# Scaling the softmax numerators of a two-layer transformer kernel on ScalarE in place of VectorE

## The reference

```python
# layer 0 attention: one head of width 1024, scores kept on and above the diagonal
q, k, v = split(x @ W)
s = triu(q @ k.T / sqrt(1024));  s = where(s == 0, -9e15, s)      # zeros are masked too
y = softmax(s) @ v
# layer 0 feed-forward: activations to 8 bits, weights ternary, GELU between
# layer 1 attention: 8 query heads of 128, 2 key/value heads, keys and values
#   through a latent of 32, causal (on and below the diagonal), output matrix wo
# layer 1 feed-forward: as in layer 0, without bias
out = x + LN(ffn1(LN(x)))
```

## Time and profile before

| | us |
|---|---|
| median of 3 runs (lowest, highest) | 11456.64 (11453.26, 11465.77) |
| profiled execution: its own time | 11503.57 |
| profiled execution: span of the slowest core, from which all rows are | 11501.7 |
| spans of the eight cores | 11419.8 to 11501.7 |
| mean granted PE clock of that core, share of 2.4 GHz | 0.691 |

### The profile page before, as it was taken

One profiled execution on the slowest core, in us unless ns is written; L12 is line 12 of the kernel. 1 busy time (PEld: TensorE's weight loads), 2 busy tenths in 40 slices (PEclk: granted clock), 3 DMA queues, 4 the chain that ended last, 5 costly groups with the idle time before them and its releaser, 6 DMA issues.

```text
span 11501.7 us, 87492 instructions; the slowest of 8 cores (11419.8 to 11501.7 us)
## 1 busy us (share of the span) xinstructions
PE 5184.4 (45%) x24204; PEld 2362.5 (21%) x24204; DVE 4585.1 (40%) x10726; ACT 3401.8 (30%) x5060; POOL 1.0 (0%) x7
## 2 busy tenths in 40 slices
PE   3444555413333325663333444455555244443666
PEld 1111222101111113331111122222222111111333
DVE  2222232234444443222234556666666422234222
ACT  1111112233444432111223333333433344443111
POOL 0000000000000000000000000000000000000000
PEclk8777766655666667886666666666666577775888
DMA  2111001141000022222000000000000311113222
GB/s 70 37 37 53 23 23 32 37 129 37 33 33 33 33 102 93 76 73 70 29 20 22 15 15 12 12 12 8 8 8 8 128 42 39 39 39 143 73 73 73
DMA packets 159419, 530.52 MB, mean 46 GB/s; under 512 B 49316, under 2 KB 65764, under 8 KB 137447
## 3 DMA queue, kind: packets, MB, share of 16 engines
q1 hardware_dynamic: 158952, 524.93, 13.4%
HBM read 373.88 MB, written 150.99 MB: 46 GB/s over the span
## 4 chain that ended last, share of the span: by engine, by line
PE 38%; DVE 24%; ACT 16%; issue 9%; DMA 6%; DVEq 3%; ACTq 3%; SPq 0%; POOL 0%; PEldq 0%; POOLq 0%
PE psO L1501 9%; PE psS L1315 8%; PE psT L165 5%; PE psS L402 4%; DVE pp L519 3%; PE psO L749 3%; DVE negmh L434 3%; PE psO L1024 3%; ACTq L1251 3%; PE psS L585 2%; DVE fam L1340 2%; ACT pp L462 2%; ACT hbuf L1375 2%; DMA wtmp<-w 2%; DVE ppT L1042 2%
## 5 line engine op out<-in xcount | busy, mean ns | idle before, releaser
L337 ACT ACT_TABLE_LOAD x128 | 164.2, 1283 | 3003.8 <-DVE st L320 3003.8
L1315 PE MATMUL psS<-wq1T,xqT 128*128 128x512 bf16 x4096 | 1031.9, 418 | 41.2 <-ACT hbuf L1369 26.5
L1501 PE MATMUL psO<-wq2T,hqT 128*128 128x512 bf16 x4096 | 1007.8, 412 | 67.3 <-DVE hqT L1486 67.3
L165 PE MATMUL psT<-identb,pp 128*128 128x128 bf16 x4752 | 538.6, 250 | 957.1 <-DVE pp L519 957.1
L165 PE MATMUL psT<-identb,xq 128*128 128x128 bf16 x512 | 64.8, 307 | 1688.8 <-DVE xq L1237 1688.8
L434 DVE TENSOR_REDUCE negmh<-psS 128x1 f32<-128x512 f32 (+3 forms) x900 | 571.7, 647 | 320.7 <-PE psS L402 303.4
L462 ACT ACTIVATE pp<-psS,negmh 128x512 bf16<-128x512 f32 (+3 forms) x900 | 580.6, 648 | 225.2 <-DVE negmh L434 215.0
L165 PEld LDWEIGHTS psT<-identb,pp 128*128 128x128 bf16 x4752 | 414.9, 112 | 1112.3 <-issue 1059.9
L402 PE MATMUL psS<-kl,qTb 128*128 128x512 bf16 (+3 forms) x792 | 393.9, 511 | 551.5 <-ACT pp L462 526.3
L1042 DVE COPY ppT<-psT 128x512 bf16<-128x512 bf16 x1056 | 448.1, 425 | 370.5 <-PE psT L165 345.8
L1315 PEld LDWEIGHTS psS<-wq1T,xqT 128*128 128x128 bf16 x4096 | 433.2, 107 | 615.7 <-issue 229.8
(11 more groups left out here) (162 smaller groups left out, 8284.8 us busy)
## 6 DMA issues: line engine op xcount, KB each, us to landing
wtmp<-w SPq DMA_DIRECT2D x128, 512.0 KB, 4.3
h_q<-hq SPq DMA_DIRECT2D x64, 1024.0 KB, 4.7
wtmp<-w SPq DMA_DIRECT2D x32, 2048.0 KB, 8.1
hqs<-h_q SPq DMA_DIRECT2D x64, 1024.0 KB, 5.8
xres<-xst SPq DMA_DIRECT2D x96, 512.0 KB, 2.9
xa<-xres SPq DMA_DIRECT2D x96, 512.0 KB, 5.5
xst<-xres SPq DMA_DIRECT2D x96, 512.0 KB, 3.8
xa<-x SPq DMA_DIRECT2D x32, 512.0 KB, 3.3
```

Source lines behind the costliest of these rows:

```text
L165: return te.matmul(out_ap, in_ap, self.identb[:], is_transpose=True, start=start, stop=stop, skip_group_check=True)
L1315: last = t.matmul(me.psS[:, hf * 512:hf * 512 + 512], B["xqTp"][:, dc * 128:dc * 128 + 128], wq1T[:, dc * HID + k * 512:dc * HID + k * 512 ...
L1501: last = t.matmul(me.psO[:, e * 512:e * 512 + 512], hqT[:, p * 4096 + hc * 128:p * 4096 + hc * 128 + 128], wq2T[:, hc * 1024 + e * 512:hc ...
```

## The change

The multiplication of `fac` by `rden` and the scaling of `pp` move from DVE to ACT, as `activation` with the function Identity, an immediate bias of 0 and a per-partition scale read from SBUF. The reciprocal now raises `v`, ACT waits for that count, and ACT's last scaling raises `s`. `flash_rows` hands back which semaphore and which count say that `pp` is ready, and the transposes wait for these. The number of instructions, their shapes, and the tiles that they read and write stay the same; so does everything outside this part of `flash_rows` and that wait.

```diff
+        rdone = me.cnt["v"] + 1
+
         @blk.scalar
         def _(s):
             me.w(s, "v", vdone)
             me.mark(s.activation(out=me.fac[:, 0:N], in_=me.fac[:, 0:N],
                                  func=AF.Exp, bias=0.0, scale=-1.0), "s")
-        sdone = me.cnt["s"]
+            s.wait_ge(me.semh["v"], rdone)
+            s.drain()
+            for r in range(R):
+                s.activation(out=me.fac[:, r * nb:r * nb + nb],
+                             in_=me.fac[:, r * nb:r * nb + nb],
+                             func=AF.Identity, bias=0.0,
+                             scale=me.rden[:, r:r + 1])
+            s.drain()
+            iv = None
+            for r in range(R):
+                pp_row = rows[r][1]
+                for c in range(nb):
+                    wdt = min(512, klen - 512 * c)
+                    iv = s.activation(out=pp_row[:, 512 * c:512 * c + wdt],
+                                      in_=pp_row[:, 512 * c:512 * c + wdt],
+                                      func=AF.Identity, bias=0.0,
+                                      scale=me.fac[:, r * nb + c:r * nb + c + 1])
+            me.mark(iv, "s")
+        sdone = me.cnt["s"] - 1
+        ppmark = me.cnt["s"]
...
-            v.reciprocal(out=me.rden[:, 0:R], in_=me.rden[:, 0:R])
-            v.drain()
-            for r in range(R):
-                v.tensor_scalar(out=me.fac[:, r * nb:r * nb + nb],
-                                in0=me.fac[:, r * nb:r * nb + nb],
-                                scalar1=me.rden[:, r:r + 1], scalar2=None,
-                                op0=ALU.mult)
-            v.drain()
-            iv = None
-            for r in range(R):
-                pp_row = rows[r][1]
-                for c in range(nb):
-                    wdt = min(512, klen - 512 * c)
-                    iv = v.tensor_scalar(out=pp_row[:, 512 * c:512 * c + wdt],
-                                         in0=pp_row[:, 512 * c:512 * c + wdt],
-                                         scalar1=me.fac[:, r * nb + c:r * nb + c + 1],
-                                         scalar2=None, op0=ALU.mult)
-            me.mark(iv, "v")
+            iv = v.reciprocal(out=me.rden[:, 0:R], in_=me.rden[:, 0:R])
+            assert me.mark(iv, "v") == rdone
+        return ("s", ppmark)
...
-                    self.flash_rows(
+                    ppsem, ppready = self.flash_rows(
...
-                    ppready = me.cnt["v"]
...
-                                    me.w(t, "v", ppready)
+                                    me.w(t, ppsem, ppready)
```

## The result

The change makes the kernel slower: 11902.74 us, the median of 8 runs (11887.18 to 11930.87), against 11455.94 us, the median of 8 runs of the kernel before on the same chip (11433.76 to 11484.11). The ratio is 1.0394, 95% interval 1.038 to 1.0408. The medians differ by 447 us where 460 were forecast; the time was forecast at 11,917 with a range of 11,850 to 12,040. The profiled execution has a span of 11898.9 us on its slowest core; it is only 397 us above the span of before, 11501.7 us, because the profiled execution of before lay 48 us over its median.

A forecast was written before the change was run, and what follows sets the result against it. No engine was taken as the bound, but a chain of handoffs with the scaling bare on it. Scaling 432, rescaling 20 and handoff 7 made 460 us more (rounded), on 11456.6: 11,917 us, range 11,850 to 12,040.

The forecast's parts named there:

- The scaling stands alone: Scaling of pp before the transposes: bare path, PE and ACT idle meanwhile; DVE's 334.6 us all lie on the path.
- The price of a step: Scaling of pp on ACT: 0.62 us from start to start, 767 us in all, 432 us more than on DVE.
- The Trainium skill's price: Scaling of pp on ACT, priced by the skill's page: 613 ns a block, an end at about 11,907 us.
- The small terms: Rescaling of fac on ACT, 20 us more, and the handoff from DVE's reciprocal to ACT, 7 us more.
- No table load: Identity on ACT needs no table load; the rival load would add 123 us, 12,040 us, chance 0.04.
- no clock: Transposes after the longer pause: no clock cost; the rival of PE staying at 1.2 GHz gave 12,147 us, chance 0.02.
- One sign: Transposes of the last call: PE would show 1.2 GHz (0.50) for 5 to 6 us, then 2.4 GHz (1.00).
- The overlap: Successive scalings on ACT overlap; the rival without overlap had a step of 0.722 us and 12,039 us, chance 0.06.
- The other side: Rival at the transposes: PE released while ACT still scales, about 11,150 us if fully hidden, chance 0.01.
- the turning point: In the early-release rival: it decides once 460 of ACT's 767 us are hidden, 60%.

The follow-up runs named there:

- e3_no_scaling: The changed kernel with the scaling of pp and the drain before it left out (computes something else): 11137.09 us, 0.9728 of the kernel before.
- e2_no_pointer: The changed kernel with an immediate scale of 1.0 instead of the pointer into fac (computes something else): 11771.86 us, 1.0287 of the kernel before.
- e1_fac_dve: The changed kernel with the small rescaling of fac back on DVE, the scaling of pp still on ACT: 11869.30 us, 1.0369 of the kernel before.
- e5_early_dve: The kernel before, scaling on DVE by column block ahead of its copies, each transpose group waiting for its own block: 11413.92 us, ratio 0.9973.

## Why the prediction was right

**The scaling stands alone.** It said that every microsecond of the step is bare path because nobody has anything else to do. The wait grew by 447.5 us and the medians by 447, and e3_no_scaling gave the other proof: 766.0 us of wait gone, and 758 to 766 us of time with it.

**The price of a step.** The prediction took 0.62 us from rows of other functions with other sources; it is 0.613. The term is 759.4 us for 767, and 425 us more than on DVE for 432. Two small errors stand behind the step, and partly cancel: one scaling lasts 709 ns for 722, because the GELU row gave 629 ns without a pointer where Identity on bf16 takes 615, and neighbours overlap by 709 - 613 = 96 ns where the sum had 722 - 620 = 102. The pointer's 93 ns were right, for one scaling (709 - 615 = 94) and in the chain (613 - 520 = 93 in e2_no_pointer). The Trainium skill's price, from its page ScalarE: Activation LUTs, section What ACT_TABLE_LOAD costs, was 613 ns a step, and the estimate by it an end at about 11,907 us. The trace agrees with the step to the nanosecond, and the estimate is 4 us off.

**The small terms.** Rescaling and handoff were put at 27 us. The wait's 447.5 less the 425 of the scaling leaves 22 to 23: the rescaling took 65.3 us on ACT for 46.9 on DVE, 18 us more where 20 were forecast, and some 4 are left for the handoff, where 7 were. e1_fac_dve returned 20.0 us of wait for both. The terms were slightly too high, by 7 us for the scaling and by 4 to 5 for the small ones; with the rounding that is the 13 us by which the sum is above the measured difference.

**No table load, no clock.** 96 loads at each of the two lines, as before. One sign was not met as written: the stretch at 1.2 GHz in the last call is 3.5 us after a pause of 27.1 us, where 5 to 6 were named from the 6.0 after 15.5. The prediction had read two calls, and single calls vary from about 3 to above 6 us in both kernels. What it rested on holds: over all phases of layer 1 the time at 1.2 GHz went from 292 to 301 us, and the phases have the same length within 3 us, all by the medians of the cores. Both rivals were dropped by the trace alone, the clock's by e3_no_scaling too.

**The overlap.** With no overlap the step would have been 0.709; the same tile read and written in place did not stop it.

**The other side.** The rival that PE might be let go early did not occur, for the reason given. Built on purpose it showed its worth: at 0.9907 with ACT's scaling the rival's mechanism is real. 580 of the 766 us were hidden there, 76% where 60% was named as the turning point. Its price of 11,150 us was too low, because it let nothing of the first block show; with the first block on DVE 11,230 was reached.

## What to carry to other kernels

Ask of a step not which engine has room for it but what runs beside it: on a chain of handoffs with nothing beside it, an engine that is 10 points less busy is worth nothing and its longer step counts in full. The same instructions on the same engine became a gain when the consumer waited for its own block and not for the last one, because then DVE's copies and ACT's scalings lay side by side. Early release alone is not enough when the consumer's next helper is queued behind the producer on one engine: then the wait only moves, as in e5_early_dve.

## What the hardware showed beside this

DVE and ACT, both reading and writing bf16 blocks of one SBUF tile at the same time, kept their steps of 0.263 and 0.613 us. PE's time at 1.2 GHz after a pause hardly grew with the pause: over the phases of layer 1 it was 292 us with pauses of 723 us in all and 301 us with 1116 us. In e5_early_dve, where PE made eight transposes and then stood still for 6.57 us, the clock stayed at 1.2 GHz through that second pause (0.50 from 8793.60 to 8800.00) and for some 4 us of work behind it.
